# More matmuls of ones ahead of and between the first products of a two-layer adapter and FFN kernel

## What is computed

```
h  = relu(x @ W1[lang] + b1[lang]);   a = x + h @ W2[lang] + b2[lang]
z  = norm(a) * gamma[lang] + beta[lang]
x  = x + bitlinear(gelu(bitlinear(z, W1, b1)), W2, b2)
y  = x @ W[subj].T + b[subj]
x  = x + bitlinear(silu(conv3(bitlinear(y, w1))), w2)
```

## Time and profile before

| | |
|---|---|
| median of 3 runs | 310.78 us (310.08 to 310.79) |
| the profiled execution | 310.48 us |
| its span, from the first to the last instruction | 308.3 us |
| PE busy | 275.0 us (89%) |
| DVE busy | 264.1 us (86%) |
| POOL busy | 251.5 us (82%) |
| ACT busy | 240.2 us (78%) |
| mean granted clock of PE | 0.945 |

### The profile page before, as it was taken

How to read it: one execution, slowest core, us unless ns; L and a number is a source line. 1 busy time by engine, 2 the same in 40 slices (tenths; PEclk the granted TensorE clock), 3 DMA queues, 4 the chain that set the end, 5 groups by cost and what they waited for, 6 DMA issues and landing times.

```text
span 308.3 us, 6480 instructions
## 1 busy us (share of the span) xinstructions
PE 275.0 (89%) x1740; PEld 188.9 (61%) x1740; DVE 264.1 (86%) x623; ACT 240.2 (78%) x367; POOL 251.5 (82%) x403
## 2 busy tenths in 40 slices
PE   6689979999999999999888987999999999696765
PEld 6336336566575666767656666677767767464643
DVE  0556797999999999678999989999999999989851
ACT  3647999989979686666668877989999898979760
POOL 2454898888889898899999999989989898997310
PEclk9755699999999999999999999999999999979987
DMA  7969685998545344551501243653453345425663
GB/s 227 261 188 376 150 220 110 164 224 222 83 110 102 70 92 81 103 105 34 105 1 34 70 86 85 104 139 82 85 131 65 87 102 91 113 54 115 142 151 90
DMA packets 88517, 37.42 MB, mean 121 GB/s; under 512 B 72805, under 2 KB 85913, under 8 KB 88482
## 3 DMA queue, kind: packets, MB, share of 16 engines
q1 hardware_dynamic: 82304, 28.40, 42.7%
q10 hardware_dynamic: 6178, 8.62, 9.5%
HBM read 16.03 MB, written 4.19 MB: 66 GB/s over the span
## 4 chain that ended last, share of the span: by engine, by line
PE 43%; DVE 25%; issue 17%; POOL 7%; ACT 4%; DMA 3%; DVEq 1%; SPq 0%; POOLq 0%; ACTq 0%
PE banks L1246 8%; PE banks L1260 8%; DVE raw_all L1033 5%; PE banks L1204 5%; DVE am L1039 5%; PE banks L1301 4%; DVE apad L1026 4%; PE banks L1247 4%; PE banks L1215 4%; PE banks L1338 2%; POOL mid L806 2%; DVE xs L1057 2%; DMA affine<-in_beta 2%; PE banks L1366 2%; POOL raw_all L813 2%
## 5 line engine op out<-in xcount | busy, mean ns | idle before, releaser
L813 POOL TENSOR_TENSOR raw_all<-raw_all,mid 128x1024 f32<-128x1024 f32 x32 | 63.6, 2014 | 1.3 <-DVE raw_all L1033 1.3
L595 ACT ACTIVATE banks<-apad,taps 128x512 f32<-128x512 f32 x64 | 42.8, 688 | 10.7 <-DVE apad L1026 10.5
L806 POOL TENSOR_SCALAR mid<-apad,taps,convb 128x512 f32<-128x512 f32 x64 | 49.0, 784 | 0.4 <-DVE apad L1026 0.4
L1033 DVE SCALAR_TENSOR_TENSOR raw_all<-apad,taps,banks 128x512 f32<-128x512 f32 x64 | 46.1, 736 | 0.0
L1366 PE MATMUL banks<-tern,q1T 128*128 128x256 bf16 x256 | 36.3, 289 | 8.6 <-DMA q1T<-r 4.3
L1026 DVE TENSOR_TENSOR apad<-banks,dqb 128x512 f32<-128x512 f32 x64 | 41.5, 679 | 2.1 <-PE banks L1338 2.0
L978 DVE TENSOR_REDUCE am<-g 128x1 f32<-128x1024 f32 x32 | 38.8, 1212 | 4.5 <-ACT g L551 4.1
L1039 DVE TENSOR_REDUCE am<-g 128x1 f32<-128x1024 f32 x32 | 38.5, 1204 | 3.7 <-ACT g L604 3.7
L551 ACT ACTIVATE g<-banks,dqz 128x1024 f32<-128x1024 f32 x32 | 35.6, 1112 | 6.8 <-PE banks L1247 3.8
L604 ACT ACTIVATE g<-banks 128x1024 f32<-128x1024 f32 x32 | 32.5, 1017 | 8.8 <-PE banks L1351 8.3
L1246 PE MATMUL banks<-tern,qT 128*128 128x512 bf16 x128 | 38.5, 383 | 0.0
(11 more groups left out here) (123 smaller groups left out, 559.6 us busy)
## 6 DMA issues: line engine op xcount, KB each, us to landing
out_y<-xs SPq DMA_DIRECT2D x32, 128.0 KB, 2.0
xs<-in_x ACTq DMA_DIRECT2D x7, 512.0 KB, 5.6
x2T<-in_xT ACTq DMA_DIRECT2D x4, 512.0 KB, 4.0
wl<-in_cwl SPq DMA_DIRECT2D x8, 256.0 KB, 2.9
xT<-in_xT ACTq DMA_DIRECT2D x3, 512.0 KB, 5.7
raw_all<-in_w1a ACTq DMA_DIRECT2D x1, 1024.0 KB, 5.8
cw<-in_cw SPq DMA_DIRECT2D x16, 64.0 KB, 4.1
raw_all<-in_w2a SPq DMA_DIRECT2D x1, 1024.0 KB, 6.1
```

The source lines that it names most:

```text
L595: act.activation(bank(BANK_U[g % 3]), apad[:, f, 2:S + 2], ACT.Copy, scale=taps[:, f, 2:3]).then_inc(p_last, 1)
L806: pool.tensor_scalar(mid[f // 2 % 2][:, f % 2, :], apad[:, f, 1:S + 1], taps[:, f, 1:2], convb[:, f:f + 1], ALU.mult, ALU.add).then_inc(p_ ...
L813: pool.tensor_tensor(c[:, 2 * q:2 * q + 2, :], c[:, 2 * q:2 * q + 2, :], mid[q % 2][:, :, :], ALU.add).then_inc(p_sum, 1)
L1033: dve.scalar_tensor_tensor(out=conv[b % 2][:, f, :], in0=apad[:, f, 0:S], scalar=taps[:, f, 0:1], in1=bank(BANK_U[(KH * b + f) % 3]), op0= ...
```

## The change

The 14 matmuls ahead of the first product become a function `keep_busy(n)`, which issues n of the same matmuls of ones, now into the bank BANK_DN in place of BANK_UP + 3. `first()` on PE calls it with 28 ahead of weight_total(0), and seven times more: with 4 behind adapter_in(0), 3 behind adapter_out(0, 0), 5 behind adapter_out(0, 1), and 3 behind each of adapter_in(1), adapter_out(1, 0), adapter_out(1, 1) and adapter_in(2). These are 24 matmuls, 48 passes. The order of all other steps stays, on every engine.

```diff
--- before.py
+++ after.py
@@ -1161,8 +1161,9 @@
             pe.wait_ge(s_ones, 1)
             pe.wait_ge(s_hone, 1)
 
-            for _ in range(14):
-                pe.matmul(bank(BANK_UP + 3)[:, 0:P], ones[:, :], ones[:, :], start=True, stop=True)
+            def keep_busy(n):
+                for _ in range(n):
+                    pe.matmul(bank(BANK_DN)[:, 0:P], ones[:, :], ones[:, :], start=True, stop=True)
 
             batches, totals = [], []
 
@@ -1393,9 +1394,10 @@
 
 
             def first():
-                weight_total(0); affine_columns(); adapter_in(0); adapter_out(0, 0); affine_rows(0); adapter_out(0, 1)
-                adapter_in(1); weight_total(1); adapter_out(1, 0); affine_rows(1); adapter_out(1, 1)
-                transpose_z(0, 0); adapter_in(2); up1(0, 0); transpose_z(0, 1); adapter_out(2, 0); up1(0, 1)
+                keep_busy(28); weight_total(0); affine_columns(); adapter_in(0); keep_busy(4); adapter_out(0, 0)
+                keep_busy(3); affine_rows(0); adapter_out(0, 1); keep_busy(5); adapter_in(1); keep_busy(3)
+                weight_total(1); adapter_out(1, 0); keep_busy(3); affine_rows(1); adapter_out(1, 1); keep_busy(3)
+                transpose_z(0, 0); adapter_in(2); keep_busy(3); up1(0, 0); transpose_z(0, 1); adapter_out(2, 0); up1(0, 1)
                 affine_rows(2); transpose_z(1, 0); adapter_out(2, 1); up1(0, 2); weight_total(2); adapter_in(3)
                 up1(0, 3); transpose_z(1, 1); adapter_out(3, 0); up1(1, 0); adapter_out(3, 1); down1(0, 0); up1(1, 1)
                 down1(0, 1); weight_total(3); affine_rows(3); up1(1, 2); transpose_z(2, 0); down1(0, 2); adapter_in(4)
```

## The result

| | before | changed |
|---|---|---|
| median of 4 executions | 310.45 us (310.08 to 310.79) | 305.97 us (303.83 to 307.46) |
| ratio, with its 95% interval | | 0.986 (0.981 to 0.991) |
| the profiled execution | 310.48 us | 307.46 us |
| its span | 308.3 us | 305.7 us |
| mean granted clock in it | 0.945 | 0.976 |

The change makes the kernel 4.5 us faster by the medians; predicted were 306.7 us and a range of 305.4 to 309.6. The profile caught the slowest of the four changed executions.

The account below looks back on a forecast made before the run. A half-clock PE alternating with the vector engines bounds the set-up; 1.76 us to the tokens' landing plus VectorE's idle 2.33 make 4.1 off 310.48, so 306.4, or 306.7 as median; range 305.4 to 309.6.

Parts of the forecast that it names:

- The clock: Set-up on PE: the granted clock stays at 1.00 from 5 to 40 us, with adapter_in(0) taking 1.90 us.
- second rival: Set-up: clock falls again, near 18.4 us; still down at adapter_in(2), gelu(0, 0) some 1.8 us late, 312.6 us; chance 0.12.
- VectorE's idle 2.33 us: Wait before add_adapted(1, 0) goes whole, worth 2.33 us, so that step starts 4.09 us earlier.
- the bank: Ones write layer 0's down bank, first otherwise used by down1(0, 0) far behind the last group: no added wait, cost 0.
- the four later groups: Groups behind adapter_in(1), adapter_out(1, 0), adapter_out(1, 1) and adapter_in(2) lie before what waits for other work: cost 0.
- The transfer: Tokens' second half lands at 17.5 us and releases add_adapted(0, 1) then instead of at 19.26: a gain of 1.76 us.
- first rival: Set-up: the tokens' second half or weight 2 lands late, only 2.33 us or less remain, 308.2 to 309 us; chance 0.12.
- The bound of 16.55: If the tokens landed earlier, add_adapted(0, 1) would start at 16.55, right behind PE, another 0.95 us early.
- The ones' overrun: Before the first product: 28 ones end at 9.54 us, so weight_total(0) starts 0.55 us late; bounds 0 to 3.5 us.
- the cover that the prediction named: VectorE's ternary(0) has room: it stood 2.80 us ahead of add_adapted(0, 0) and needs 0.55 + 1.7.
- The rule against it: Set-up: transposes don't count as busy for the full clock, so quiet places grow from about 1.0 to some 1.5 us.
- third rival: Behind 44 us: loads or DMA transposes, not PE, set the pace and the gain is given back, 310.6 us; chance 0.06.

Follow-up runs that it names:

- the change again: The unmodified change measured once more against the kernel before: median 307.22 us, ratio 0.986.
- 20 ones: The change with 20 instead of 28 ones ahead of weight_total(0), the seven groups kept: median 307.45 us, ratio 0.990 to the kernel before.
- three at the end: The change plus 8 ones ahead of the last batch's fourth up and 3 ahead of each of five late down2: 303.80 us, ratio 0.980 to the kernel before.
- 42 ones: The change with 42 instead of 28 ones ahead of weight_total(0), the seven groups kept: median 309.38 us, ratio 1.004 to the kernel before.
- groups only: The change with the old 14 ones ahead of weight_total(0), the seven groups kept: median 308.48 us, ratio 0.994 to the kernel before.
- six in a group: The change plus 8 ones ahead of the last batch's fourth up and 6 ahead of each of five late down2: 305.66 us, ratio 0.991.
- three with the tokens early: On the version with three at the end, the tokens' second half issued ahead of weight 1 on SP: 304.17 us, ratio 0.979 to the kernel before.

## Why the prediction was right

The forecast came in sign and mechanism: with PE at full clock the idle time of VectorE goes, and the set-up ends 3.5 to 3.9 us early where 4.1 was forecast. That the whole time came so near is partly luck.

- **The clock** held through the set-up in both profiles of the change, up to 267 us. The second rival's fall can be seen with the groups taken out (16.2 to 23.0 us). Even then it isn't slower than before: the clock is back before adapter_in(2), which was the condition that the rival named, and the groups, whose cost that rival counts, are not there.
- **Which part holds it** the prediction did not ask. It gave the longer prefix as the start of the chain, with add_adapted(0, 0) 1.7 us early. With 14 ones and the groups that step is 0.28 us early in the profile, and gelu(0, 0) comes as early as with 28: add_adapted(0, 1), which waits for the tokens or for PE until about 18 us in either case, hides the difference.
- **VectorE's idle 2.33 us** went whole, and the bank and the four later groups cost nothing that shows; doubling the groups brings that idle time back. VectorE was not unbroken, though: it waits 0.23 us for POOL behind the late bias_rest, and add_adapted(1, 0) is 3.60 us early in place of 4.09.
- **The transfer** is where the first rival's mechanism does appear, at the size of a term: add_adapted(0, 1) came at 18.45, 18.25 and 17.98 in three profiles where the tokens released it (the change again, 20 ones, three at the end), and at 17.86 in the first, where the overrun of the ones did, instead of 17.5. So the term is 0.8 to 1.4 us and not 1.76. The bound of 16.55, "right behind PE", came when the tokens were issued earlier; that it is met to the hundredth is chance.
- **gelu(0, 0)** was forecast at about 32.2 and came at 32.35 and 32.73. In the first of them ScalarE made up for part of what was lost ahead of it: from squares(1, 0) to gelu(0, 0) it took 8.16 us instead of 8.52.
- **The ones' overrun** was sized wrongly. 0.55 us assumed that the clock rises as early as in the profile of before (4.8 us). In the profile of the change the ones took 9.32 us, in the repeat 7.84, so weight_total(0) was 1.83 and 0.36 late. It cost little, for the cover that the prediction named held: VectorE's room, and the tokens. 42 ones show the cover's end.
- **The end** was sized wrongly too. "The tail, where the clock falls again, can shift by some tenths": from adapter_in(3) to the end the two profiles of the change differ by 1.6 us, and whole executions of it by 6.0 (303.8 to 309.8), of the kernel before by 8.0 (305.6 to 313.7). "0.3% from no change" is finer than a few such executions allow. The median of the result's four, 305.97, and that of all ten, 306.74, stand on both sides of 306.7. Two things move the end, a transpose's 3.1 to 5.1 us and the half clock. With ones near the end as well the time was lower by another 2 to 3 us, of which the prediction had nothing.
- **The rule against it**: the place with transposes and then a wait, 25.6 to 27.2 us, did grow (PE waits 1.03 us there, for a load), and the clock stayed, so the fall that the prediction worked out from the rule did not come. The Trainium skill (TensorE: Matmul & The Clock Gate, Part 4: PE-mode transpose) says that transposes don't count as busy in the same way; no run here isolates that.
- **Given back**, the third rival, holds in part and not always: in the profiled execution 1.2 us of it went to a DMA transpose, which that rival named, in the repeat nothing did.
- **Slips of the working** that change little: the stretch from 34 to 36 us with its 0.63 puts the return of the full clock at 35.5 and not 35.2; 13 ones in 1.61 us, counted as the prediction counts, are 0.115 us apart and not 0.111 (the groups do run at 0.111); the range's lower end leaves out the 0.3 us that the forecast adds for the median; and the chances as split give 0.09 for the same time and 0.09 for slower.

## What to carry to other kernels

Where PE alternates with other engines in short steps, look at the granted clock by stretch before anything else; if it stands at 0.50 on a path that PE's products end, matmuls that nobody reads, put into waits that are there anyway and into a bank that is free, can buy the full clock. Size each group to the wait that it fills: without them the clock was lost (16.2 to 23.0 us), with twice as many they were on the path (gelu(0, 0) 3.05 us later). Test the parts alone: here the groups with the old prefix already had the set-up's gain up to gelu(0, 0). Look for every stretch at half clock, not only the first: by the medians the end of this kernel was worth about as much as its beginning.

## What was not expected of the hardware

- **The clock's rise moves.** With the same 28 ones, it came at 7.46, 4.37, 5.96, 7.30, 5.37, 5.33 and 4.36 us in seven profiles. The Trainium skill (TensorE: Matmul & The Clock Gate, Part 1) says that the number of matmuls at the low clock differs from run to run of one kernel; these rows agree.
- **One wait's length doesn't tell whether the clock falls.** A wait of 2.06 us ahead of adapter_in(3) stands in thirteen profiles, of before and after too. The clock fell there in one of them (groups only, at 41.6 us) and with 42 ones, where the wait was 2.45 (at 43.8). With the groups out it fell behind waits of 0.77 and 0.52 us.
- **The same kernel's time varies with it.** The ten executions of the change differ by 2% (303.8 to 309.8 us), in step with their time at half clock. The spread is 2.3, 2.8 and 2.0 us in three versions with ones near the end (six in a group, three, three with the tokens early), but 4.4 with 20 ones ahead and 6.0 on the kernel before; and without them it is 2.7, 1.8 and 2.6 with 20 and 42 ones and with the groups doubled. So that ones near the end narrow it isn't shown.
